# Four reorderings in the attention stages of a one-core gated block: row statistics, bias copies, |w| sums and row normalisation

## The chip, the cores and the metric

The kernel runs on one core of a Trainium2 chip. The metric is the device time of one execution in microseconds (us), as the median of several runs. Engines are named as in the profile: PE (TensorE matmul), PEld (its weight load), DVE (VectorE), ACT (ScalarE), POOL (GpSimd) and SP (SyncE, which here only issues DMAs).

## The reference, cut to what matters

```python
x = x + tanh(g_xattn[0]) * xattn(layernorm(x), ctx, Wq, bq, Wk, bk)
x = x + tanh(g_ffn[0]) * ffn(layernorm(x), W_up, W_gate, W_down)

def xattn(t, ctx, Wq, bq, Wk, bk):        # t: (4, 512, 512), ctx: (4, 512, 256)
    q = einsum('bnc,dc->bnd', ctx, Wq) + bq
    k = einsum('bnc,dc->bnd', ctx, Wk) + bk
    attention = softmax(einsum('bnd,bmd->bnm', q, k), axis=-1)
    return einsum('bln,bmn->blm', t, attention)

def ffn(x, W_up, W_gate, W_down):         # 512 -> 2048 -> 512
    # ternary(w): scale = mean(|w|) + 1e-8; clip(round(w / scale), -1, 1) * scale
    up, gate = x @ ternary(W_up).T, x @ ternary(W_gate).T
    return (silu(up) * gate) @ ternary(W_down).T
```

## The kernel before, in words

There are four batches of 512 rows by 512 columns. A row tile is 128 rows, so a batch has four (NT = 4). Everything up to about 95 us is attention; from there on PE runs the products of the feed-forward part back to back. All five engines have their instructions written out by hand in program order, and semaphores tie them together. What is reordered is therefore only what one engine does next.

Attention of one batch goes like this. `project(b, m)` (L736, PE) makes queries (m = 0) and keys (m = 1) in PSUM. `bias_qk(b, m)` (L1109, ACT) adds the bias and copies them to SBUF. `energy(b, i)` (L750, PE) is one row tile of energies. `row_max` (L1487, DVE), `exp_row` (L1116, ACT), `row_rsum` (L1491, DVE) and `norm_p` (L1121, ACT; in batch 0 tiles 1 to 3 on DVE, L1573, counted by `s_pn0`) make the softmax. `transpose_p` (L761, PE) turns the probabilities round and `copy_at` (L1125, ACT) copies them to SBUF, counted by `s_at`.

The product of x with the attention is done in two ways.

- Batches 0 and 1: by seven block products instead of eight, `mix_product(b, j)` (L800, PE) in the order j = 1, 2, 6, 5, 7, 3, 4, each of four matmuls (eight records). Three of them take blocks as they are (1, 2, 4 on the left side), the others take sums of blocks. POOL makes these sums: four "x sums" (L574 to L583, counted by `s_ss`) and four "attention sums" `p_sum_1` to `p_sum_4` (L587 to L598, counted by `s_ts`). Product 6 needs an x sum and the second attention sum, product 7 an x sum and the third attention sum. `XA` says which x sum a product takes, and so for which count of `s_ss` it waits. `add_mixed(b, j)` (L1521, DVE) scales a product by the row's 1/sigma and adds it to x. PE's product 6 waits for `add_mixed(b, 1)`.
- Batches 2 and 3: plainly, one row tile after another, `mix(b, i)` (L777, PE, four matmuls, which the trace records as eight) and `make_x1(b, i)` (L1509, DVE).

The row statistics of the first layer norm are `bn_stats` and `bn_aggr` on DVE (L1498, L1504, counted by `s_ln1`) and then on POOL `rstd1_two(b, h)` for two row tiles at once (L559 to L563, five small instructions with a wait after each, counted by `s_r1`) or `rstd1(b, i)` for one (L549 to L552). Those of the second layer norm are `stats2`, `aggregate2` (L1529, L1535) on DVE and `rstd2_two` or `rstd2` on POOL (L568, L569; L603, L604). `norm_x1(b, i)` (L1543, DVE) normalises a row tile for the feed-forward part; it waits for `rstd2` of that tile.

Beside this ACT sums |w| over the weights, `sum_abs(m, c)` (L1102, 2048 columns each), as their DMAs land. DVE also makes the low parts of the feed-forward's input, `low_t` (L1561).

The program order before, around the change:

- POOL, batch 0: x sums 0 and 1; then, after `s_pn0` = 3, the third x sum; `p_sum_1`, `rstd1_two(0, 0)`, `p_sum_2`, `rstd1_two(0, 1)`, `p_sum_3`, the fourth x sum, `p_sum_4`; then the x sums of batch 1.
- ACT, batch 0: `copy_at(0, 3)`, `bias_qk(1, 0)`, `bias_qk(1, 1)`, `sum_abs(0, 0)`, `sum_abs(0, 1)`, the exponentials of batch 1's tiles 0 and 1, their two `norm_p`, `sum_abs(0, 2)`, `copy_at(1, 0)`, `exp_row(1, 2)` and so on.
- PE, batch 0: ..., `transpose_p(0, 3)`, product 1, `energy(1, 0)`, `energy(1, 1)`, product 2, product 6, `transpose_p(1, 0)`, `energy(1, 2)`, products 5 and 7, `transpose_p(1, 1)`, `energy(1, 3)`, product 3, ...
- DVE, batch 0: `add_mixed(0, 1)`, `row_max` and `row_rsum` of batch 1's tiles 0 and 1, `add_mixed(0, 2)`, ...
- DVE, batches 2 and 3, for each tile i: `make_x1(b, i)`, `stats2`, `row_max` of the next batch, `aggregate2`, `stats1` of a later tile, `row_rsum`, `aggregate1`, and in batch 2 `norm_x1(2, i)`; then a `low_t` or a subtraction.
- PE, batch 2: `mix(2, 1)`, `transpose_p(3, 0)`, `energy(3, 2)`, `mix(2, 2)`, `transpose_p(3, 1)`, `energy(3, 3)`, `transpose_p(3, 2)`, `mix(2, 3)`, `transpose_p(3, 3)`, then `mix(3, 0)` to `mix(3, 3)`.

`energy(b, 1)` and `transpose_p(0, 3)` use the same PSUM bank.

Of the kernel before, what the change touches and what calls it, by code (L numbers as in the profile page):

```python
# [6 lines left out]
def gated_block_kernel(nc, x, xT, first, ctxT, wqkT, wugT, wdT, x1_dram, out):  # L7
# [19 lines left out]
    NT = ROWS // P  # L27
# [18 lines left out]
    with stack:  # L46
# [207 lines left out]
        XA = {1: (0, 0), 2: (0, 1), 4: (1, 1), 5: 0, 7: 1, 6: 2, 3: 3}  # L254
# [266 lines left out]
        def _(pool):  # L521
# [49 lines left out]
            def x_sums_1(b):  # L571
                for i in range(NT):
                    pool.wait_ge(*xt_in(b, i))
                pool.tensor_tensor(x_sum(b, 0), x_quarter(b, 1, 0), x_quarter(b, 1, 1), ALU.add).then_inc(s_ss, 1)  # L574
                pool.tensor_tensor(x_sum(b, 1), x_quarter(b, 0, 0), x_quarter(b, 1, 0), ALU.subtract).then_inc(s_ss, 1)

            def x_sum_2(b):
                hold(pool, s_ss, 4 * b + 1)
                pool.tensor_tensor(x_sum(b, 2), x_sum(b, 0), x_quarter(b, 0, 0), ALU.subtract).then_inc(s_ss, 1)

            def x_sum_4(b):
                hold(pool, s_ss, 4 * b + 3)
                pool.tensor_tensor(x_sum(b, 3), x_quarter(b, 0, 1), x_sum(b, 2), ALU.subtract).then_inc(s_ss, 1)  # L583
# [41 lines left out]
            x_sums_1(0)  # L625
            hold(pool, s_pn0, NT - 1)
            x_sum_2(0)
            p_sum_1(0)
            rstd1_two(0, 0)
            p_sum_2(0)  # L630
            rstd1_two(0, 1)
            p_sum_3(0)
            x_sum_4(0)
            p_sum_4(0)
            x_sums_1(1)
            x_sum_2(1)
            x_sum_4(1)
# [93 lines left out]
        def _(pe):  # L731
# [8 lines left out]
            def energy(b, i):  # L740
                if b == 0 and i == 0:
                    pe.wait_ge(s_k0, 2)
                    pe.wait_ge(s_q0, 1)
                elif b == 0 and i == 1:
                    pe.wait_ge(s_qk, 2)
                elif i == 0:
                    pe.wait_ge(s_qk, b * 2 + 2)
                if i >= 2 and b > 0:
                    pe.wait_ge(s_exp, b * NT + i - 1)
# [340 lines left out]
        def _(act):  # L1090
# [86 lines left out]
            for b in range(NB):  # L1177
                first, last = b == 0, b == NB - 1
                copy_at(b, NT - 1)
# [4 lines left out]
                else:  # L1184
                    bias_qk(b + 1, 0)
                    bias_qk(b + 1, 1)
                if first:
                    sum_abs(0, 0)
                    sum_abs(0, 1)
# [6 lines left out]
                for i in range(NT):  # L1196
# [25 lines left out]
                    if first and i in (0, NT - 1):  # L1222
                        sum_abs(0, 2 + (i > 0))
# [260 lines left out]
        def _(dve):  # L1484
# [142 lines left out]
            for b in range(NS, NB):  # L1627
                last = b == NB - 1
                for i in range(NT):
# [21 lines left out]
                    if not last:  # L1651
                        norm_x1(b, i)
# [9 lines left out]
                    if last:  # L1662
                        if i == 0:
                            low_t(0, "T2", xf_half(0, 0))
# [308 lines left out]
```

## Time and profile before

| what | us |
|---|---|
| median of 3 runs | 396.75 (396.34 to 397.29) |
| the profiled execution, its own time | 397.67 |
| its span, first to last instruction | 395.9 |
| PE busy in the span | 390.0 |
| DVE / ACT / POOL busy | 314.5 / 266.7 / 170.4 |

The profiled execution took 0.9 us more than the median, and 1.8 us of its time lie outside the span. Busy time of PE is modelled from the starts of its matmuls, so a group's end reaches into the next one's start; what PE loses is best read as the distance between starts.

### The profile page before, as it was taken

The page shows a single profiled execution, that of the slowest core. Times are in us where ns is not written, and L with a number is a line of the kernel's source. Part 1 is how long each engine was busy: PE and PEld are TensorE (multiplying, and loading weights), DVE is VectorE, ACT ScalarE, POOL GpSimd, SP SyncE. Part 2 cuts the span into 40 slices and gives each one's busy share as a digit, 9 for nine tenths or more (in the row PEclk, how much of TensorE's full clock was granted, in tenths as well). Part 3 has the DMA queues.
Part 4 walks back from the last instruction along what each step waited for, and adds up shares of the span by engine and source line. Part 5 has one row for each costly group of instructions (what it writes and reads, how often), then busy time and mean ns, then how long its engine had stood idle before and what let it go on. Part 6 is the DMA issues. An engine that isn't in the chain of part 4 may idle for free.

```text
span 395.9 us, 6059 instructions
## 1 busy us (share of the span) xinstructions
PE 390.0 (99%) x1944; PEld 214.8 (54%) x1952; DVE 314.5 (79%) x475; ACT 266.7 (67%) x360; POOL 170.4 (43%) x187
## 2 busy tenths in 40 slices
PE   8999999999999999999999999999999999999997
PEld 6567775454444444444444444444445565656886
DVE  0768898788889985779897875786869989798974
ACT  3796989789778686868887863746377566654400
POOL 0487826658985014222337001535359446271000
PEclk9999999999999999999999999999999999999999
DMA  7999967599600030030009643041500000000014
GB/s 278 410 412 415 392 208 161 150 270 224 157 9 0 1 108 0 0 108 0 2 0 219 117 81 65 1 160 74 170 23 1 2 2 2 0 2 0 2 54 160
DMA packets 43183, 43.91 MB, mean 111 GB/s; under 512 B 30992, under 2 KB 33168, under 8 KB 41104
## 3 DMA queue, kind: packets, MB, share of 16 engines
q1 hardware_dynamic: 43152, 43.53, 35.6%
q8 instruction: 16, 0.26, 0.3%
q14 instruction: 15, 0.12, 0.1%
HBM read 29.89 MB, written 6.29 MB: 91 GB/s over the span
## 4 chain that ended last, share of the span: by engine, by line
PE 82%; ACT 6%; DVE 4%; issue 4%; POOL 3%; DMA 1%; DVEq 0%; POOLq 0%; ACTq 0%
PE pair L886 23%; PE pair L888 22%; PE pair L960 14%; PE pair L1004 11%; PE pair L777 4%; PE pair L800 2%; PE pair L750 2%; PE pair L736 2%; ACT sh L1116 1%; PE pair L761 1%; PE pair L815 1%; DMA xf<-in_first 1%; DVE x_sb L1521 1%; ACT sh L1121 1%; DVE small L1487 1%
## 5 line engine op out<-in xcount | busy, mean ns | idle before, releaser
L886 PE MATMUL pair<-xb_hi,w_sb 128*128 128x512 f16 x448 | 169.8, 379 | 0.2 <-DVE xf L1683 0.2
L888 PE MATMUL pair<-xb_lo,w_sb 128*128 128x512 f16 x448 | 169.8, 379 | 0.0
L886 PEld LDWEIGHTS pair<-xb_hi,w_sb 128*128 128x128 bf16 x448 | 43.8, 98 | 52.4 <-ACT xf L1313 0.7
L888 PEld LDWEIGHTS pair<-xb_lo,w_sb 128*128 128x128 bf16 x448 | 43.9, 98 | 51.2 <-issue 0.3
L1264 ACT ACTIVATE xf<-xf,small 128x512 f32<-128x512 f32 x48 | 34.5, 720 | 52.4 <-DVE xf L1683 31.6
L960 PE MATMUL pair<-x_sb,sh 128*128 128x512 bf16 x248 | 55.0, 379 | 0.4
L1688 DVE SCALAR_TENSOR_TENSOR xf<-xf,small 128x512 f32<-128x512 f32 x48 | 40.1, 837 | 8.4 <-ACT xf L1264 8.3
L960 PEld LDWEIGHTS pair<-x_sb,sh 128*128 128x128 f16 x256 | 24.9, 98 | 30.6 <-DVE x_sb L1725 0.8
L610 POOL TENSOR_TENSOR w_sb<-w_sb 128x512 bf16<-128x512 bf16 x8 | 9.6, 1196 | 63.1 <-ACT w_sb L1138 63.1
L1693 DVE TENSOR_TENSOR sh<-xf,sh 128x512 f16<-128x512 f32 x36 | 32.1, 900 | 0.7 <-ACT sh L1275 0.7
L1739 DVE SCALAR_TENSOR_TENSOR x_sb<-pair,small,x_sb 128x256 f32<-128x256 f32 (+1 forms) x57 | 25.6, 475 | 5.9 <-PE pair L1004 5.4
L1725 DVE SCALAR_TENSOR_TENSOR x_sb<-pair,small,x_sb 128x512 f32<-128x512 f32 x32 | 23.9, 748 | 7.8 <-PE pair L960 7.7
L1275 ACT ACTIVATE sh<-xf 128x512 f16<-128x512 f32 x36 | 22.1, 623 | 10.4 <-DVE xf L1688 9.2
L709 POOL TENSOR_TENSOR xf<-xf 128x512 f32<-128x512 f32 x7 | 9.8, 1406 | 44.2 <-DMA xb_lo<-xf 28.1
L777 PE MATMUL pair<-sh,xt_sb 128*128 128x512 f32 (+2 forms) x80 | 28.6, 509 | 0.0
L1678 DVE TENSOR_TENSOR xf<-pair,xf 128x1024 f32<-128x1024 f32 x16 | 19.5, 1221 | 8.8 <-PE pair L888 8.6
L1683 DVE TENSOR_TENSOR xf<-pair,xf 128x1024 f32<-128x1024 f32 x16 | 19.5, 1221 | 4.1 <-PE pair L888 3.9
L1673 DVE TENSOR_TENSOR xf<-pair,xf 128x1024 f32<-128x1024 f32 x16 | 19.5, 1221 | 4.1 <-issue 1.6
L1301 ACT ACTIVATE xf<-pair 128x1024 f32<-128x1024 f32 x16 | 16.4, 1022 | 8.1 <-PE pair L888 7.7
L777 PEld LDWEIGHTS pair<-sh,xt_sb 128*128 128x128 f32 x80 | 13.9, 190 | 12.6 <-issue 10.5
L1688 DVE SCALAR_TENSOR_TENSOR c<-c,small,pair 128x512 f32<-128x512 f32 x16 | 11.9, 742 | 10.1 <-ACT c L1264 10.1
L1132 ACT ACTIVATE w_sb<-w_sb,small 128x1024 f32<-128x1024 f32 x16 | 18.9, 1227 | 0.0
(198 smaller groups left out, 717.3 us busy)
## 6 DMA issues: line engine op xcount, KB each, us to landing
w_sb<-in_wugT SPq DMA_DIRECT2D x8, 1024.0 KB, 15.4
x_sb<-in_x SPq DMA_DIRECT2D x4, 1024.0 KB, 11.6
xf<-in_wdT SPq DMA_DIRECT2D x4, 1024.0 KB, 6.6
xt_sb<-in_wdT SPq DMA_DIRECT2D x4, 1024.0 KB, 5.2
xt_sb<-in_xT SPq DMA_DIRECT2D x12, 256.0 KB, 6.3
x_dram<-x_sb SPq DMA_DIRECT2D x8, 256.0 KB, 3.4
out<-x_sb SPq DMA_DIRECT2D x8, 256.0 KB, 2.0
x_sb<-x_dram SPq DMA_DIRECT2D x2, 1024.0 KB, 5.5
```

Source lines behind the costliest of these rows:

```text
L777: last = pe.matmul(ps_x[i % 2][:, lo:hi], xt_tile(b, i)[:, k, :], at[:, k, lo:hi], start=(k == 0), stop=(k == KD - 1))
L886: pe.matmul(dst[:, m * 512:(m + 1) * 512], w[:, o:o + P], hi[:, k], start=start and k == 0, stop=False, skip_group_check=not start)
L888: last = pe.matmul(dst[:, m * 512:(m + 1) * 512], w[:, o:o + P], lo[:, k], start=False, stop=k == 1, skip_group_check=not start)
L960: ins = pe.matmul(dst, h_part(n, c, lo)[:, i * P:(i + 1) * P], t_d[:, e * DM + lo_col:e * DM + hi_col], start=first and n == units[0] and ...
L1004: ins = pe.matmul(fin_bank(g, j, t), hidden(u, c, lo, min(t, NT - 1)), cols, start=first and u == units[0] and lo == 0 and not (side and t ...
L1264: act.activation(cb(n, c)[:, 0:512], src, ACT.Silu, scale=su[:, :]).then_inc(s_silu[c], 1)
L1275: act.activation(part(n, c, 0), shaped(n, c, cb(n, c)[:, 0:512]), ACT.Copy).then_inc(s_hi[c], 1)
L1673: dve.tensor_tensor(cb(n, "11"), ps_y[:, :], cb(n, "11"), ALU.add).then_inc(s_c["11"], 1)
L1688: dve.scalar_tensor_tensor(cb(n, c)[:, 0:512], cb(n, c)[:, 0:512], kap[:, :], gate, ALU.mult, ALU.mult).then_inc(s_mul[c], 1)
L1693: dve.tensor_tensor(part(n, c, 1), shaped(n, c, cb(n, c)[:, 0:512]), part(n, c, 0), ALU.subtract)\
L1725: dve.scalar_tensor_tensor(y_tile(b, i), at, c_out[:, :], y_tile(b, i), ALU.mult, ALU.add)\
L1739: dve.scalar_tensor_tensor(fin_rows(g, j, t), fin_bank(g, j, t), c_out[:, :], fin_rows(g, j, t), ALU.mult, ALU.add).then_inc(s_ef, 1)
```

## The change

Four things are moved. Nothing is computed that was not computed before.

1. POOL, batch 0: `rstd1_two(0, 0)` stands ahead of `p_sum_1(0)` instead of behind it. The four x sums are split into four functions: the difference of the two plain blocks, which was second, is now third, and in batch 0 it is done behind `rstd1_two(0, 1)` instead of at the very beginning. `XA` and the semaphore counts follow the new order. In batch 1 the same four sums stand in the new order.
2. ACT, batch 0: both `bias_qk(1, m)` stand ahead of `copy_at(0, 3)`. Because of the shared PSUM bank PE waits at `energy(1, 1)` for `s_at` = 4.
3. ACT, batch 0: `sum_abs(0, 1)` moves from ahead of the exponentials of batch 1's tiles 0 and 1 to behind their `norm_p`, where it stands ahead of `sum_abs(0, 2)`.
4. DVE, batch 2: `norm_x1(2, i)` is done one tile later, at the place of tile i + 1; the last one in batch 3 at tile 0.

```diff
--- before.py
+++ after.py
@@ -251,7 +251,7 @@
         MIX = (1, 2, 6, 5, 7, 3, 4)
         MIX_TO = {1: (0, 0), 5: (1, 1), 6: (0, 1), 3: (0, 1), 7: (1, 1), 2: (0, 0), 4: (1, 0)}
         MIX_BEFORE = {2: 1, 3: 6, 7: 5}
-        XA = {1: (0, 0), 2: (0, 1), 4: (1, 1), 5: 0, 7: 1, 6: 2, 3: 3}
+        XA = {1: (0, 0), 2: (0, 1), 4: (1, 1), 5: 0, 6: 1, 7: 2, 3: 3}
         PB = {1: (0, 0), 2: (1, 0), 3: (1, 1), 5: 0, 6: 1, 7: 2, 4: 3}
 
         def x_quarter(b, lh, nh):
@@ -568,19 +568,21 @@
                 step(pool.tensor_scalar(ve2[:, two], mv2[:, own, 1], LN_EPS, 1.0 / XS ** 2, ALU.add, ALU.mult))
                 pool.tensor_tensor(r2[:, own], ve2[:, two], mhalf, ALU.pow).then_inc(s_r2, 2)
 
-            def x_sums_1(b):
+            def x_sum_1(b):
                 for i in range(NT):
                     pool.wait_ge(*xt_in(b, i))
                 pool.tensor_tensor(x_sum(b, 0), x_quarter(b, 1, 0), x_quarter(b, 1, 1), ALU.add).then_inc(s_ss, 1)
-                pool.tensor_tensor(x_sum(b, 1), x_quarter(b, 0, 0), x_quarter(b, 1, 0), ALU.subtract).then_inc(s_ss, 1)
 
             def x_sum_2(b):
                 hold(pool, s_ss, 4 * b + 1)
-                pool.tensor_tensor(x_sum(b, 2), x_sum(b, 0), x_quarter(b, 0, 0), ALU.subtract).then_inc(s_ss, 1)
+                pool.tensor_tensor(x_sum(b, 1), x_sum(b, 0), x_quarter(b, 0, 0), ALU.subtract).then_inc(s_ss, 1)
+
+            def x_sum_3(b):
+                pool.tensor_tensor(x_sum(b, 2), x_quarter(b, 0, 0), x_quarter(b, 1, 0), ALU.subtract).then_inc(s_ss, 1)
 
             def x_sum_4(b):
-                hold(pool, s_ss, 4 * b + 3)
-                pool.tensor_tensor(x_sum(b, 3), x_quarter(b, 0, 1), x_sum(b, 2), ALU.subtract).then_inc(s_ss, 1)
+                hold(pool, s_ss, 4 * b + 2)
+                pool.tensor_tensor(x_sum(b, 3), x_quarter(b, 0, 1), x_sum(b, 1), ALU.subtract).then_inc(s_ss, 1)
 
             def p_sum_1(b):
                 hold(pool, s_at, b * NT + NT)
@@ -622,18 +624,20 @@
 
             pool.wait_ge(s_tanh, 1)
             pool.wait_ge(s_const, 4)
-            x_sums_1(0)
+            x_sum_1(0)
             hold(pool, s_pn0, NT - 1)
             x_sum_2(0)
+            rstd1_two(0, 0)
             p_sum_1(0)
-            rstd1_two(0, 0)
             p_sum_2(0)
             rstd1_two(0, 1)
+            x_sum_3(0)
             p_sum_3(0)
             x_sum_4(0)
             p_sum_4(0)
-            x_sums_1(1)
+            x_sum_1(1)
             x_sum_2(1)
+            x_sum_3(1)
             x_sum_4(1)
             rstd1_two(1, 0)
             rstd2_two(0, 0)
@@ -745,6 +749,8 @@
                     pe.wait_ge(s_qk, 2)
                 elif i == 0:
                     pe.wait_ge(s_qk, b * 2 + 2)
+                if b == 1 and i == 1:
+                    pe.wait_ge(s_at, NT)
                 if i >= 2 and b > 0:
                     pe.wait_ge(s_exp, b * NT + i - 1)
                 pe.matmul(e_bank(b, i), q_sb[:, i * P:(i + 1) * P], k_sb, start=True, stop=True).then_inc(s_e, 1)
@@ -1176,17 +1182,19 @@
 
             for b in range(NB):
                 first, last = b == 0, b == NB - 1
+                if first:
+                    bias_qk(1, 0)
+                    bias_qk(1, 1)
                 copy_at(b, NT - 1)
                 if last:
                     act.activation(warm[:, :], tanh_sb[:, :], ACT.Silu)
                     sign_unit(0)
                     sum_abs(2, 3)
-                else:
+                elif not first:
                     bias_qk(b + 1, 0)
                     bias_qk(b + 1, 1)
                 if first:
                     sum_abs(0, 0)
-                    sum_abs(0, 1)
                 elif not last:
                     if b == 1:
                         sum_abs(1, 0)
@@ -1219,8 +1227,11 @@
                             act.wait_ge(s_t1, 1)
                             high_t(0, "T1", xf_half(1, 0))
 
-                    if first and i in (0, NT - 1):
-                        sum_abs(0, 2 + (i > 0))
+                    if first and i == 0:
+                        sum_abs(0, 1)
+                        sum_abs(0, 2)
+                    if first and i == NT - 1:
+                        sum_abs(0, 3)
                     if b == 1:
                         if i == 0:
                             sum_abs(1, 2)
@@ -1648,8 +1659,8 @@
                         row_rsum(b + 1, i + 1)
                     if more:
                         aggregate1(nb, ni, mark1)
-                    if not last:
-                        norm_x1(b, i)
+                    if not last and i > 0:
+                        norm_x1(b, i - 1)
                     if b == 2:
                         if i == 1:
                             low_t(0, "T3", t3_sb)
@@ -1661,6 +1672,7 @@
                             dve.tensor_tensor(xf_half(0, 0), t3_sb, xf_half(0, 0), ALU.add).then_inc(s_t2, 1)
                     if last:
                         if i == 0:
+                            norm_x1(b - 1, NT - 1)
                             low_t(0, "T2", xf_half(0, 0))
                         if i == 1:
                             low_t(0, "B22", xf_half(1, 1))
```

## Rows read from the trace of the kernel before

**Rows 1.** The page of the profile, busy time of each engine.

```profile
PE 390.0 (99%) x1944; PEld 214.8 (54%) x1952; DVE 314.5 (79%) x475; ACT 266.7 (67%) x360; POOL 170.4 (43%) x187
```

**Rows 2.** Timeline of PE, attention of batches 0 and 1: start, length, what, idle.

```profile
17.79 1.89 PE L800 MATMUL pair<-sh,xt_sb 128*128 128x256 f32 x8
19.79 1.98 PE L750 MATMUL pair<-sh 128*128 128x512 f32 x4
...
23.66 1.97 PE L800 MATMUL pair<-xf 128*128 128x256 f32 x8 [0.16 <-POOL xf L591]
26.07 0.66 PE L761 MATMUL pair<-early,sh 128*128 128x128 f32 x4 [0.44 <-ACT sh L1121]
26.56 1.02 PE L750 MATMUL pair<-sh 128*128 128x512 f32 x2
...
39.94 1.89 PE L800 MATMUL pair<-sh,xb_lo 128*128 128x256 f32 x8
...
47.27 1.02 PE L750 MATMUL pair<-sh 128*128 128x512 f32 x2
```

**Rows 3.** Timeline of PE, attention of batches 2 and 3.

```profile
66.01 3.60 PE L777 MATMUL pair<-sh,xt_sb 128*128 128x512 f32 x8
...
70.74 3.60 PE L777 MATMUL pair<-sh,xt_sb 128*128 128x512 f32 x8
...
74.61 1.02 PE L750 MATMUL pair<-sh 128*128 128x512 f32 x2
...
75.91 3.60 PE L777 MATMUL pair<-sh,xt_sb 128*128 128x512 f32 x8
80.25 0.66 PE L761 MATMUL pair<-early,sh 128*128 128x128 f32 x4 [0.74 <-ACT sh L1121]
80.75 10.51 PE L777 MATMUL pair<-sh,xt_sb 128*128 128x384 f32 x32
```

**Rows 4.** Timeline of POOL, first batch.

```profile
16.06 1.27 POOL L579 TENSOR_TENSOR xf<-xf,xt_sb 128x512 f32<-128x512 f32 x1 [2.76 <-DVE sh L1573]
18.73 1.27 POOL L587 TENSOR_TENSOR xf<-sh 128x512 f32<-128x512 f32 x1 [1.40 <-ACT sh L1125]
20.08 0.19 POOL L559 TENSOR_SCALAR small<-small 128x2 f32<-128x2 f32 x1
...
22.24 1.28 POOL L591 TENSOR_TENSOR xf<-sh,xf 128x512 f32<-128x512 f32 x1
```

**Rows 5.** Timeline of ACT, first batch.

```profile
17.98 0.60 ACT L1125 ACTIVATE sh<-pair 128x512 f32<-128x512 f32 x1 [1.45 <-PE pair L761]
...
19.62 1.92 ACT L1102 ACTIVATE xb_hi<-w_sb 128x2048 f16<-128x2048 f32 x1
...
23.96 0.69 ACT L1116 ACTIVATE sh<-pair,small 128x512 f32<-128x512 f32 x1 [0.44 <-DVE small L1487]
```

**Rows 6.** Timeline of DVE, first batch.

```profile
17.43 0.18 DVE L1504 BATCH_NORM_AGGREGATE small<-small 128x2 f32<-128x6 f32 x1
...
22.39 0.88 DVE L1521 SCALAR_TENSOR_TENSOR x_sb<-pair,small,x_sb 128x256 f32<-128x256 f32 x2 [3.05 <-POOL small L563]
```

**Rows 7.** Timeline of POOL beside the third batch.

```profile
70.96 0.63 POOL L550 TENSOR_TENSOR small<-small 128x1 f32<-128x1 f32 x1
...
75.23 1.34 POOL L550 TENSOR_TENSOR small<-small 128x1 f32<-128x1 f32 x1
```

**Rows 8.** Timeline of DVE, third and fourth batch.

```profile
70.63 0.55 DVE L1543 TENSOR_SCALAR xf<-x_sb,small 128x512 f32<-128x512 f32 x1 [2.07 <-POOL small L604]
71.09 0.74 DVE L1509 SCALAR_TENSOR_TENSOR x_sb<-pair,small,x_sb 128x512 f32<-128x512 f32 x1
...
74.95 1.22 DVE L1561 TENSOR_TENSOR xb_lo<-t_sb,xb_hi 128x1024 f16<-128x1024 f32 x1
...
95.33 0.75 DVE L1509 SCALAR_TENSOR_TENSOR x_sb<-pair,small,x_sb 128x512 f32<-128x512 f32 x1
```

**Rows 9.** Timeline of ACT, end of the third batch.

```profile
79.48 0.72 ACT L1121 ACTIVATE sh<-sh,small 128x512 f32<-128x512 f32 x1
```

## Prediction

> **What bounds the kernel now.** I read the page first. PE is busy for 99% of the span [rows 1], so only what lets PE lose less can help, and the question is where PE loses anything. The list of PE's waits names few; all but the one at the start lie between 23 and 81 us, where this change is made. Because the ends of matmuls are modelled, I then read the loss from distances between starts in PE's timeline.
>
> Batches 0 and 1 run the same sequence: product 1, two energies, product 2, product 6, a transpose, the next energy. In batch 1 it takes 47.27 - 39.94 = 7.33 us without a wait, in batch 0 it takes 26.56 - 17.79 = 8.77 us [rows 2]. So batch 0 loses 1.44 us. Its parts: a product or an energy pair takes (7.33 - 0.44) / 4 = 1.72 us (0.44 for a transpose is my estimate, the 0.49 from 26.07 to 26.56 less a little for its start after a wait), so the energies at 19.79 come 0.28 late; the transpose and what is marked at it and at product 6 make the rest.
>
> In batch 2 a mix, a transpose and the start of the next energy take 74.61 - 70.74 = 3.87 us; the same from 75.91 (mix, transpose, start of the next mix) takes 80.75 - 75.91 = 4.84 us [rows 3]. That is 0.97 us lost, waiting for `norm_p(3, 3)` [rows 9]. Together 2.41 us can come back.
>
> **The bias copies.** The energies at 19.79 wait for both `bias_qk(1, m)`, which stand behind `copy_at(0, 3)`; ACT had idled 1.45 us before that copy [rows 5]. Moved ahead, the first copy of the biases fits into that idle time, the second must wait for its projection, which ends at about 17.5, just before product 1's first matmul [rows 2]; both are done by 18.2, `copy_at(0, 3)` by 18.8 instead of 18.6. PE wants the energies at 17.79 + 1.72 = 19.51. The new wait for `s_at` = 4 at `energy(1, 1)` is met at 18.8, so it costs nothing; all of PE stands behind it, and it would cost only if the copy came after 20.4. Gain: the 0.28 us.
>
> **The statistics ahead of the sums.** POOL idled 1.40 us before `p_sum_1`, from 17.33 on [rows 4]. `rstd1_two(0, 0)` needs only the second tile's aggregate, ready at 17.43 + 0.18 = 17.61 [rows 6]; with 0.16 us of hand-over (my estimate, the size of the waits tagged in rows 2) it starts at 17.77 instead of 20.08. From its first instruction to the next function is 22.24 - 20.08 = 2.16 us, to DVE's `add_mixed(0, 1)` 22.39 - 20.08 = 2.31 us [rows 4, 6]. So:
>
> - `add_mixed(0, 1)` starts at 20.08 (product 1 ended by then). The exponential follows 23.96 - 22.39 = 1.57 us later [rows 5, 6], at 21.65, and PE's transpose 26.07 - 23.96 = 2.11 us after that, ready at 23.76.
> - `p_sum_1` starts at 17.77 + 2.16 = 19.93, a good us after `copy_at(0, 3)` has let it, and takes 1.27; with 0.14 for the wait on itself `p_sum_2` starts at 21.34, ends at 22.62 and reaches PE 0.14 later (22.24 + 1.28 against 23.66), at 22.76.
> - PE wants product 6 at 17.79 + 3 x 1.72 = 22.95 and the transpose at 24.67. Both are met, with 0.2 and 0.9 us in hand.
>
> So the whole 1.44 us comes back. What is late next is product 7. PE wants it at 24.67 + 0.44 + 0.86 + 1.72 = 27.69 (half a pair for one energy). POOL: `p_sum_2` ends at 22.62, the second `rstd1_two` takes 2.16 and about 0.1 of start, then the moved x sum and `p_sum_3` at 1.24 to 1.27 each: done at 27.4, at PE by 27.5. It also holds, by 0.2 us. Before, this x sum had been done in POOL's first idle time, so it now costs POOL 1.25 us that the 1.1 us saved in front pay for; batch 1's sums are needed only after 40 us and hide that.
>
> If a small POOL instruction stretches, both margins go. The nearest rows are the same one-column power at 0.63 and at 1.34 us [rows 7], 0.71 more. One such stretch ahead of product 6 costs 0.71 - 0.2 = 0.5 us; two ahead of product 7 cost 1.42 - 0.2 = 1.2 us, which is the bound above. Below, nothing: POOL cannot give PE more than PE can take. I take no stretch, since the row of 1.34 ran beside DVE's `low_t` [rows 7, 8], and in 17.8 to 27.5 DVE runs `bn_stats`, `row_max` and `add_mixed`, no such subtraction.
>
> The Trainium skill (SBUF — State Buffer, section "SBUF: two separate sides") says that DVE and GpSimd share a port pair that one of them holds for a whole instruction, DVE only in its two-port modes or with two SBUF inputs; by that rule the two stretches would be 0 and the sum as I have it. The pair of rows at 75 us agrees (1.34 us beside a subtraction of two SBUF operands).
>
> **The |w| sum behind the exponentials.** It runs 1.92 us plus 0.2 for its read-out [rows 5]. Before, two such sums stood ahead of the exponentials. With the exponential wanted at 21.65 the second, started at 20.6, would have held ACT until 22.7; moved, it isn't in the way. It and `sum_abs(0, 2)` then fill ACT from 24.3 to 28.2; behind them are queued `copy_at(1, 0)`, the third exponential and its `norm_p`, done by 31. PE wants them at the third transpose, 27.69 + 1.72 + 0.44 + 0.86 + 1.72 = 32.4. Cost nothing, with 1.4 us of cover.
>
> **The later normalisation.** DVE idled 2.07 us ahead of `norm_x1(2, 0)`, waiting for POOL's `rstd2`; `make_x1(2, 1)` stood behind it at 71.09 [rows 8]. Without it, it can start when `mix(2, 1)` ends, 66.01 + 3.60 = 69.61 [rows 3]: 1.44 us earlier (69.65). The chain behind it on DVE and ACT (statistics, `row_max`, exponential, `low_t`) is as long as before, one norm standing in each round as it did, so `norm_p(3, 3)` starts at 79.48 - 1.44 = 78.04 and ends at 78.76. PE wants its transpose 3.43 us after 75.91, at 79.34. Gain 0.97 us, with 0.5 in hand. (Times of this paragraph are on the old axis; all of it lies 1.44 earlier by then.) The fourth batch has one norm more, 71.09 - 70.63 = 0.46 us; DVE brings 1.44 with it, so `make_x1(3, 3)`, now at 95.33, still follows PE's last mix, which comes 0.97 earlier. If DVE gained only 0.5 net, product 3 of the first feed-forward unit, which hangs on it by two ACT copies and shows no slack that I can measure from a wait, would take back up to 0.5 us.
>
> **The sum.** 1.44 + 0.97 = 2.41 us. Against the profiled execution's 397.67 us that is 395.3 (span 393.5); the median is 0.92 us below it: 396.75 - 2.41 = 394.34. I say 394.4.
>
> **Rivals.**
>
> - *POOL late:* a stretched power costs 0.5 to 1.2 us at products 6 or 7. For it: margins of only 0.2 us, and a row of 1.34. Against it: no `low_t` on DVE there. Time 394.9 to 395.6.
> - *The stall at the third batch stays*, or moves to `make_x1(3, 3)`: DVE is then bound by something else than the norm. For it: DVE was 79% busy. Against it: 2.07 us of idle time are marked. Only 1.44 come: 395.3.
> - *No change:* both gains are met by waits next in line, or the shift is taken up by the |w| and x loads, which come at fixed times of the DMA queues. Against it: batch 1 ran its sequence without loss, and ACT and DVE found those loads landed. 396.75, within 0.8.
> - *Slower, one mechanism:* POOL's sums of 512 columns themselves stretch now that they meet DVE at other moments. If the four from `p_sum_1`'s start to product 7 took 1.27 + 0.71 us, product 7 would come 4 x 0.71 - 0.2 = 2.6 us late, and products 3 and 4 behind two more sums another 1.4 us: 396.75 - 2.41 + 4.0 = 398.3. It decides from 0.6 us of stretch per sum on. Against it: all sums in rows 4 take 1.27 or 1.28.
>
> **How the numbers follow.** The measurement tells 0.2% (0.8 us) from no change. Chances: full gain 0.58, POOL late 0.15, third-batch stall stays 0.11, no change 0.10, slower 0.06. The first three hold 0.84; they reach from 394.34 less half the runs' spread (0.45) to 395.6. Range 393.9 to 395.7. Faster by over 0.2% (under 395.96): 0.84; within: 0.10; slower: 0.06.
>
> **What would show it.** In PE's timeline of the changed kernel the batch-0 sequence should take 7.3 to 7.4 us, and the mix before `transpose_p(3, 3)` to the next mix 3.9. POOL's L559 should start near 17.8, DVE's first L1521 near 20.1, ACT's first exponential of batch 1 near 21.7, L1509 of tile (2, 1) right after the mix. The prediction is wrong if PE shows a wait for POOL's L591 or L594, if L1138 to L1313 on ACT or L1509 on DVE hold up PE near 100 us, or if PE's first feed-forward product does not start 2.4 us earlier than now.

## The result and the profile after

The changed kernel takes 394.2 us (393.69 to 394.87) against 396.75 us (396.34 to 397.29), each the median of 5 runs: ratio 0.9935, 95% interval 0.9917 to 0.9953, so 2.55 us less, with 2.41 worked out and 394.4 predicted. Its profiled execution took 393.74 us, with a span of 391.9. Line numbers from L574 on differ by a few from before's (L604 is L606, L736 is L740, L750 is L756, L761 is L767, L777 is L783, L800 is L806, L1102 is L1108, L1109 is L1115, L1116 is L1122, L1121 is L1127, L1125 is L1131, L1313 is L1324, L1487 is L1498, L1504 is L1515, L1509 is L1520, L1521 is L1532, L1543 is L1554, L1561 is L1572; for POOL, L579 is L578, L587 is L589, L591 is L593, L594 is L596).

The page's busy times, the row that answers to [rows 1]:

```profile
PE 388.1 (99%) x1952; PEld 214.4 (55%) x1952; DVE 315.7 (81%) x475; ACT 266.5 (68%) x360; POOL 168.6 (43%) x187
```

PE's timeline in the changed kernel, batches 0 and 1, then the third batch:

```profile
16.44 1.89 PE L806 MATMUL pair<-sh,xt_sb 128*128 128x256 f32 x8
18.17 1.88 PE L756 MATMUL pair<-sh 128*128 128x512 f32 x4
...
21.61 1.89 PE L806 MATMUL pair<-xf 128*128 128x256 f32 x8
23.34 0.60 PE L767 MATMUL pair<-early,sh 128*128 128x128 f32 x4
23.77 1.02 PE L756 MATMUL pair<-sh 128*128 128x512 f32 x2
...
73.12 3.60 PE L783 MATMUL pair<-sh,xt_sb 128*128 128x512 f32 x8
76.56 0.60 PE L767 MATMUL pair<-early,sh 128*128 128x128 f32 x4
76.99 1.46 PE L783 MATMUL pair<-sh,xt_sb 128*128 128x384 f32 x4
```

Against [rows 2]: product 1 to the next energy takes 23.77 - 16.44 = 7.33 us, where it took 8.77. No row of the sequence carries a wait any more. Against [rows 3]: the mix at 73.12, a transpose and the start of the next mix take 76.99 - 73.12 = 3.87 us, where they took 4.84. Both stretches are now as long as their undisturbed twins. That is 1.44 + 0.97 = 2.41 us. PE's first feed-forward product starts 90.99 - 16.44 = 74.55 us behind product 1, where it started 94.75 - 17.79 = 76.96 us behind it: again 2.41 us, so no part of the gain is lost on the way there, and no PE row of the sequence or of the third batch names POOL.

The profiled spans differ by 4.0 us, so 1.6 are not the change's. 1.35 of them are the start: product 1 begins at 16.44 instead of 17.79. In the fourteen executions profiled here it began anywhere from 16.44 to 17.80. The two profiles of the unchanged kernel before have 17.79 and 17.75, but variants of it, with the same PE program, also began at 16.78 to 17.00, and variants of the changed kernel at up to 17.80. PE's timeline shows where the 1.35 come from, first in the changed kernel, then in the kernel before:

```profile
3.85 2.21 PE L821 MATMUL pair<-xf 128*128 128x256 f32 x8
```

```profile
3.98 3.42 PE L815 MATMUL pair<-xf 128*128 128x256 f32 x8
```

It is the same work, the first half of the first projections, and PE has been busy since 0.97 us. Before, its weight loads took 335 ns each (median), in the changed kernel 192. PE runs the beginning at half its later pace, with starts of 256-column records 0.43 us apart instead of 0.22, and over the profiles this ends anywhere from 4 to 7 us. The profile lists the granted clock as 1.00 there all the same, so it doesn't name the cause. The first energies start at 9.10 before and 7.75 here, and that is the 1.35.

Distances from product 1's start can be compared, absolute times can't. The last 0.2 lie in the feed-forward part, and I come back to them.

POOL, first batch, against [rows 4]:

```profile
16.30 0.20 POOL L559 TENSOR_SCALAR small<-small 128x2 f32<-128x2 f32 x1 [0.45 <-DVE small L1515]
...
18.47 1.27 POOL L589 TENSOR_TENSOR xf<-sh 128x512 f32<-128x512 f32 x1
19.89 1.27 POOL L593 TENSOR_TENSOR xf<-sh,xf 128x512 f32<-128x512 f32 x1
...
24.64 1.28 POOL L596 TENSOR_TENSOR xf<-sh 128x512 f32<-128x512 f32 x1
```

ACT, first batch and end of the third, against [rows 5] and [rows 9]:

```profile
16.20 0.69 ACT L1115 ACTIVATE sh<-pair,small 128x512 f32<-128x512 f32 x1 [0.44 <-PE pair L740]
16.79 0.59 ACT L1131 ACTIVATE sh<-pair 128x512 f32<-128x512 f32 x1
...
20.19 0.69 ACT L1122 ACTIVATE sh<-pair,small 128x512 f32<-128x512 f32 x1 [0.93 <-DVE small L1498]
...
22.77 1.90 ACT L1108 ACTIVATE xb_lo<-w_sb 128x2048 f16<-128x2048 f32 x1
...
75.25 0.72 ACT L1127 ACTIVATE sh<-sh,small 128x512 f32<-128x512 f32 x1
```

DVE, first and third batch, against [rows 6] and [rows 8]:

```profile
18.62 0.88 DVE L1532 SCALAR_TENSOR_TENSOR x_sb<-pair,small,x_sb 128x256 f32<-128x256 f32 x2 [0.77 <-POOL small L563]
...
66.86 0.75 DVE L1520 SCALAR_TENSOR_TENSOR x_sb<-pair,small,x_sb 128x512 f32<-128x512 f32 x1 [1.09 <-PE pair L783]
```

Measured from product 1's start, the prediction and the rows compare so:

| step | predicted | measured |
|---|---|---|
| `rstd1_two(0, 0)`, first instruction | -0.02 | 16.30 - 16.44 = -0.14 |
| `add_mixed(0, 1)` | 2.29 | 18.62 - 16.44 = 2.18 |
| first exponential of batch 1 | 3.86 | 20.19 - 16.44 = 3.75 |
| second attention sum done, with hand-over | 4.97 | 19.89 + 1.27 + 0.14 - 16.44 = 4.86 |
| product 6 | 5.16 | 21.61 - 16.44 = 5.17 |
| third attention sum's margin at product 7 | 0.2 | 21.61 + 1.73 + 0.43 + 0.86 + 1.73 - (24.64 + 1.28 + 0.14) = 0.3 |
| last `norm_p` of the third batch to PE's transpose | 0.5 (its times give 79.34 - 78.76 = 0.58) | 76.56 - (75.25 + 0.72) = 0.6 |

The second projection's bias copy starts at 16.20, 0.24 ahead of product 1, and `copy_at(0, 3)` follows at 16.79; the energies at 18.17 come 1.73 behind product 1, with nothing lost. `make_x1(2, 1)` (66.86) now waits for PE's mix, and for nothing of POOL's.

### The profile page after: what moved, and what is told of

It reads as the page before. It is cut to its first block, busy times and chain, and to the rows that moved or that the text cites. A ratio compares the mean times of both kernels' runs of the same rounds, so it can differ in the third digit from the quotient of the medians.

```text
span 391.9 us, 6067 instructions
## 1 busy us (share of the span) xinstructions
PE 388.1 (99%) x1952; PEld 214.4 (55%) x1952; DVE 315.7 (81%) x475; ACT 266.5 (68%) x360; POOL 168.6 (43%) x187
## 4 chain that ended last, share of the span: by engine, by line
PE 94%; DVE 2%; issue 2%; ACT 1%; POOL 0%; DVEq 0%; POOLq 0%; ACTq 0%
PE pair L892 23%; PE pair L894 23%; PE pair L966 14%; PE pair L1010 11%; PE pair L783 7%; PE pair L806 6%; PE pair L756 4%; PE pair L740 3%; PE pair L767 2%; PE pair L817 1%; DVE xf L1700 1%; PE pair L821 1%; DVE x_sb L1751 0%; PE pair L825 0%; POOL xf L717 0%
## 5 line engine op out<-in xcount | busy, mean ns | idle before, releaser
L966 PE MATMUL pair<-x_sb,sh 128*128 128x512 bf16 x256 | 56.6, 379 | 0.0
L783 PE MATMUL pair<-sh,xt_sb 128*128 128x512 f32 (+2 forms) x80 | 28.6, 509 | 0.0
L783 PEld LDWEIGHTS pair<-sh,xt_sb 128*128 128x128 f32 x80 | 13.9, 190 | 12.6 <-issue 10.5
```

Source lines behind the costliest of these rows:

```text
L783: last = pe.matmul(ps_x[i % 2][:, lo:hi], xt_tile(b, i)[:, k, :], at[:, k, lo:hi], start=(k == 0), stop=(k == KD - 1))
L966: ins = pe.matmul(dst, h_part(n, c, lo)[:, i * P:(i + 1) * P], t_d[:, e * DM + lo_col:e * DM + hi_col], start=first and n == units[0] and ...
```

## The experiments

What follows are runs of variants. The first four ran on one chip, where the kernel before took 396.75 us (29 runs); the next four on another (397.63, 9 runs); the last four on a third (396.52, 29 runs). Each was timed in five rounds beside the kernel before. "Sequence" is from product 1's start to `energy(1, 2)` (8.77 before, 7.33 after), "third batch" from the mix ahead of `transpose_p(3, 3)` to the next mix (4.84 and 3.87).

### One edit alone, or all but one

**Only the later normalisation**, on the kernel before:

```diff
-                    if not last:
-                        norm_x1(b, i)
+                    if not last and i > 0:
+                        norm_x1(b, i - 1)
...
+                            norm_x1(b - 1, NT - 1)
                             low_t(0, "T2", xf_half(0, 0))
```

> The kernel before with edit 4 alone (the third batch's rows normalised a tile later). Theory (the two stalls are separate and each edit removes its own): PE from the mix before transpose_p(3, 3) to the next mix takes 3.87 us instead of 4.84, the batch-0 sequence stays at 8.77, the time falls by 0.97 us. Rival (the gain of the third batch hangs on the earlier first batch): the 4.84 stays or only partly goes, the time falls by less than 0.4 us.

Measured: 396.22 us, ratio 0.9986 [0.9978, 0.9995]; third batch 3.87, sequence 9.06. So 0.53 us (0.2 to 0.9) instead of 0.97. The third batch came out as expected, the sequence longer by 0.3.

**All but the later normalisation** (the same lines turned back in the changed kernel).

> The changed kernel with norm_x1 of the third batch back in its old place. Theory: batch-0 sequence 7.33 us, the stall before transpose_p(3, 3) is back (4.84 instead of 3.87), 1.44 us faster than before and 0.97 slower than the changed kernel. Rival (an earlier first batch alone frees POOL enough): the stall at the third batch is below 0.5 us.

Measured: 394.83 us, 0.9958 [0.9941, 0.9974]; sequence 7.34, third batch 78.39 - 74.32 = 4.07. The third batch lost 0.20 us, not 0.97, without the edit that was to cure it: the number that the rival had named. Whether for its reason, the last group of runs tells.

**Only POOL's new order**, with its x sums and `XA`, on the kernel before (the lines of the x sums and of `XA` are left out here):

```diff
...
+            rstd1_two(0, 0)
             p_sum_1(0)
-            rstd1_two(0, 0)
             p_sum_2(0)
             rstd1_two(0, 1)
+            x_sum_3(0)
             p_sum_3(0)
```

> The kernel before with edit 1 alone (POOL's statistics ahead of the sums, x sums reordered). Theory (each of edits 1 to 3 removes one wait of the batch-0 sequence): add_mixed(0, 1) comes 2.3 us earlier, but ACT is held by the second |w| sum until 23.4, so the transpose comes only 0.5 us earlier: sequence 8.2 to 8.3 us, time 0.5 us lower. Rival (the statistics were all of it): sequence 7.6 us (only the 0.28 of the bias copies left), time 1.2 us lower.

Measured: 396.35 us, 0.9985 [0.9976, 0.9994]; sequence 9.20, third batch 4.82. The sequence is neither the 8.2 to 8.3 of the theory nor the 7.6 of the rival, but longer than before.

**All but POOL's new order** (POOL's program and `XA` of before in the changed kernel).

> The changed kernel with POOL's program of before (edits 2, 3 and 4 kept). Theory (POOL's order carries the batch-0 gain): add_mixed(0, 1) waits for POOL as before, the sequence takes 8.8 to 8.95 us (0.17 more than before since copy_at(0, 3) comes later), only the 0.97 of the third batch remains: time 0.8 to 1.0 us below before. Rival (ACT's order carries it): sequence under 8.0 us, time 1.7 us or more below.

Measured: 396.71 us, 0.9998 [0.9988, 1.0007]; sequence 8.92, third batch 3.87. Its PE timeline:

```profile
23.60 1.97 PE L802 MATMUL pair<-xf 128*128 128x256 f32 x8 [0.68 <-POOL xf L591]
26.01 0.66 PE L763 MATMUL pair<-early,sh 128*128 128x128 f32 x4 [0.44 <-ACT sh L1123]
```

With the statistics back behind the first sum, product 6 waits for POOL again and the transpose for ACT, though bias copies and |w| sum stand in their new places. The sequence is as expected. The profile also shows most of the expected gain: from product 1's start to the start of PE's last matmul it takes 374.00 us, against 375.01 and 374.74 in the two profiles of the kernel before. The median of its 11 runs does not: it is 0.04 us below before's where 0.8 to 1.0 were expected, and no profile says why.

The edits don't add up. Alone, normalisation and POOL order bring 0.53 and 0.40 us by the medians (0.56 and 0.60 by the ratios), both with a sequence *longer* than before's 8.77. ACT's timelines say what ended it. Only the normalisation, then only POOL's order (whose L1106 is before's L1102, L765 is L761, L804 is L800, L754 is L750):

```profile
21.57 1.91 ACT L1102 ACTIVATE xb_lo<-w_sb 128x2048 f16<-128x2048 f32 x1 [0.73 <-DMA w_sb<-in_wugT]
```

```profile
21.70 1.91 ACT L1106 ACTIVATE xb_lo<-w_sb 128x2048 f16<-128x2048 f32 x1 [0.87 <-DMA w_sb<-in_wugT]
```

And PE in the same two:

```profile
17.00 1.89 PE L800 MATMUL pair<-sh,xt_sb 128*128 128x256 f32 x8
...
26.06 1.02 PE L750 MATMUL pair<-sh 128*128 128x512 f32 x2
```

```profile
16.99 1.89 PE L804 MATMUL pair<-sh,xt_sb 128*128 128x256 f32 x8
...
25.70 0.66 PE L765 MATMUL pair<-early,sh 128*128 128x128 f32 x4 [1.27 <-ACT sh L1125]
26.19 1.02 PE L754 MATMUL pair<-sh 128*128 128x512 f32 x2
```

In both, ACT stood still ahead of the second |w| sum, not for an engine but for the DMA of its block of weights, and the exponentials were queued behind that sum. In the profile of the kernel before, product 1 began 0.8 us later, and the block had landed by the time ACT came to it. The next group tests this.

### One part of the first batch turned back

**The second |w| sum ahead of the exponentials again**, all else as changed:

```diff
                 if first:
                     sum_abs(0, 0)
+                    sum_abs(0, 1)
...
                     if first and i == 0:
-                        sum_abs(0, 1)
                         sum_abs(0, 2)
```

> The changed kernel with sum_abs(0, 1) back ahead of the exponentials of batch 1. The prediction's working: ACT is held 1.05 us longer than the exponential wants, the transpose comes 0.14 us late, sequence 7.5 us. Theory from the changed kernel's trace: the transpose has 1.1 us in hand and the sum takes 0.9 of it, so sequence 7.33 us and the same time as the changed kernel, 2.4 us faster than before. Rival (the |w| sum is what held the exponential): sequence 8 us or more.

Measured: 396.1 us, 0.9964 [0.9951, 0.9976]; sequence 26.24 - 17.05 = 9.19, third batch 3.87. ACT and PE:

```profile
21.74 1.91 ACT L1108 ACTIVATE xb_lo<-w_sb 128x2048 f16<-128x2048 f32 x1 [1.85 <-DMA w_sb<-in_wugT]
```

```profile
17.05 1.89 PE L806 MATMUL pair<-sh,xt_sb 128*128 128x256 f32 x8
...
25.75 0.66 PE L767 MATMUL pair<-early,sh 128*128 128x128 f32 x4 [1.56 <-ACT sh L1127]
26.24 1.02 PE L756 MATMUL pair<-sh 128*128 128x512 f32 x2
```

1.86 us of sequence are lost, where the prediction's working gave 0.14 and the theory of this run nothing. It is the rival, 8 us or more, and more than everything that the change gains in this batch. ACT waited 1.85 us for the landing, and the transpose 1.56 us for ACT. By time it costs less: 0.6 to 1.2 us, from 0.9964 here against 0.9948 and 0.9935 for the changed kernel on other chips. A profile is one execution, and how much the landing costs depends on how early product 1 starts.

**The bias copies behind `copy_at(0, 3)` again:**

```diff
-                if first:
-                    bias_qk(1, 0)
-                    bias_qk(1, 1)
                 copy_at(b, NT - 1)
+                if first:
+                    bias_qk(1, 0)
+                    bias_qk(1, 1)
```

> The changed kernel with both bias_qk(1, m) back behind copy_at(0, 3). Theory: the energies behind product 1 come 0.28 us late and nothing else moves: batch-0 sequence 7.6 us, 2.1 us faster than before. Rival (the slack of POOL absorbs nothing, but PE's wait is hidden because product 6 waits anyway): sequence 7.33 us.

Measured: 394.99 us, 0.9940 [0.9927, 0.9952]; third batch 3.88. PE:

```profile
17.80 1.89 PE L806 MATMUL pair<-sh,xt_sb 128*128 128x256 f32 x8
19.80 1.98 PE L756 MATMUL pair<-sh 128*128 128x512 f32 x4
21.62 1.89 PE L806 MATMUL pair<-sh,xt_sb 128*128 128x256 f32 x8
...
25.51 1.02 PE L756 MATMUL pair<-sh 128*128 128x512 f32 x2
```

The energies start 2.00 us behind product 1 instead of 1.73, and nothing makes it good later: sequence 7.71, 0.38 us more. 0.27 of it are the late start. The other 0.11 arise right behind it: the pair of energies, started after a wait, takes 21.62 - 19.80 = 1.82 us to the next product instead of 1.71 (19.88 - 18.17 in the changed kernel). In time the loss does not show: 0.9940 lies between the two ratios of the changed kernel, 0.9935 and 0.9948.

**The x difference in POOL's first idle time again**, and only `rstd1_two(0, 0)` moved ahead of `p_sum_1`. The x sums and `XA` are those of the kernel before in both batches; edits 2, 3 and 4 stay. POOL's program against the kernel before:

```diff
             x_sum_2(0)
+            rstd1_two(0, 0)
             p_sum_1(0)
-            rstd1_two(0, 0)
             p_sum_2(0)
             rstd1_two(0, 1)
```

> The changed kernel with the difference of two plain x blocks back in POOL's first idle time (and the x sums in their old order in both batches), the statistics still ahead of the attention sums. Theory: the sums for product 7 are ready 1.2 us earlier, which nobody waits for: sequence 7.33 us, time as the changed kernel, 2.4 us faster than before. Rival (product 7 has no slack): PE gains up to 0.2 us more there.

Measured: 394.11 us, 0.9917 [0.9903, 0.9930]; sequence 7.33, as in the changed kernel. So in the changed kernel POOL's margin at product 7 was enough.

**The moved x sum (1.24 us) between the statistics and `p_sum_1`:**

```diff
             rstd1_two(0, 0)
+            x_sum_3(0)
             p_sum_1(0)
             p_sum_2(0)
             rstd1_two(0, 1)
-            x_sum_3(0)
             p_sum_3(0)
```

> The changed kernel with one x sum (1.24 us of POOL) put between the statistics and p_sum_1, to use up POOL's slack at product 6. Theory (POOL's margin there is 0.3 us by the changed kernel's trace): PE waits 0.9 us at product 6, sequence 8.25 us, 1.5 us faster than before. Rival (POOL is not near the path): sequence 7.33 us.

Measured: 395.16 us, 0.9945 [0.9932, 0.9959]. PE:

```profile
16.59 1.89 PE L806 MATMUL pair<-sh,xt_sb 128*128 128x256 f32 x8
...
22.90 1.97 PE L806 MATMUL pair<-xf 128*128 128x256 f32 x8 [0.98 <-DVE x_sb L1532]
...
25.14 1.02 PE L756 MATMUL pair<-sh 128*128 128x512 f32 x2
```

Product 6 starts 22.90 - 16.59 = 6.31 us behind product 1 instead of 5.17, so it is 1.14 late (the mark says 0.98, because it counts from a modelled end). POOL was 1.24 us later for the x sum, and 0.23 more because its statistics began 0.09 behind product 1 in this execution and not 0.14 ahead of it; less the margin of 0.3 of the table above, that is 1.17. The mark names DVE's `add_mixed`, which had been done by 19.87; what came late was POOL's `p_sum_2`, from 21.49 for 1.27 us, and 0.14 of hand-over: 22.90. The sequence takes 25.14 - 16.59 = 8.55 us, 0.3 more than expected.

### Both kernels again, and the power on POOL

`all_but_norm` raised a question: why did the third batch lose 0.20 us instead of 0.97? The chain back from its `norm_x1(2, 0)` leads over POOL's `rstd2(2, 0)`, which stands behind two subtractions (L651, L653), to a two-column power on POOL, L569. The kernel before, POOL and DVE:

```profile
61.47 1.95 POOL L569 TENSOR_TENSOR small<-small 128x2 f32<-128x2 f32 x1
```

```profile
61.65 1.22 DVE L1561 TENSOR_TENSOR xb_lo<-xf,xb_hi 128x1024 f16<-128x1024 f32 x1
```

All but the normalisation, POOL and DVE:

```profile
59.89 0.81 POOL L569 TENSOR_TENSOR small<-small 128x2 f32<-128x2 f32 x1
```

```profile
60.06 1.22 DVE L1572 TENSOR_TENSOR xb_lo<-xf,xb_hi 128x1024 f16<-128x1024 f32 x1
...
68.27 0.55 DVE L1554 TENSOR_SCALAR xf<-x_sb,small 128x512 f32<-128x512 f32 x1 [1.30 <-POOL small L606]
```

The same power took 1.95 us in one and 0.81 in the other, beside the same `low_t` on DVE, which by the records starts 0.18 or 0.17 us after it. DVE then idles 1.30 us ahead of `norm_x1(2, 0)` instead of the 2.07 of [rows 8], and PE loses 0.20 instead of 0.97. Three of the remaining four runs ask whether that is the edit's doing; the last returns to the |w| sum.

**The kernel before and the changed kernel, each unchanged.**

> The kernel before, unchanged, for a second look. Theory (two things vary from execution to execution: the start of product 1, and whether POOL's power at L569 takes 0.8 or 1.95 us beside DVE's low_t): ratio 1.000, the transpose behind product 6 at 25.5 or later however early product 1 starts, since the second |w| block lands at 21.5 to 21.7, and PE from the mix to the next mix 4.84 us if the power took 1.95, about 4.1 if 0.8. Rival (the losses are fixed): batch-0 sequence 8.77 and 4.84 again.

> The changed kernel, unchanged, for its ratio on the same chip as the others of this call. Theory: sequence 7.33 and 3.87 us whatever the start and the power; 2.5 to 3 us faster than before. Rival (the profile of the changed kernel was a lucky one): 1.5 us or less.

Measured: before 396.4 us, 1.0001 [0.9993, 1.0010]; changed 394.42 us, 0.9948 [0.9936, 0.9959], so 2.1 us less. That is less than the 2.5 to 3 us expected and more than the rival's 1.5. Sequences 8.79 and 7.33, third batch 4.07 and 3.87, the power 0.81 us in both:

```profile
61.45 0.81 POOL L569 TENSOR_TENSOR small<-small 128x2 f32<-128x2 f32 x1
```

So the kernel before itself has either power, and a third batch that loses 0.97 or 0.20 us. Product 1 began as late here (17.75) as in its first profile, so an earlier first batch was not what shortened the stall in `all_but_norm`.

This profile shows a second reason for a late product 1, and here POOL's order has a hand in it. POOL and DVE:

```profile
12.23 1.27 POOL L575 TENSOR_TENSOR xf<-xt_sb 128x512 f32<-128x512 f32 x1
```

```profile
12.35 1.43 DVE L1573 TENSOR_SCALAR sh<-sh,small 128x512 f32<-128x512 f32 x1
```

DVE's `norm_p` of batch 0 takes 0.49 us when no sum of POOL's runs beside it. Here it ends 0.28 us behind POOL's x difference, the sum that the change moves away from there. PE's transpose is marked as waiting 0.35 us for it, and product 1 comes 17.75 - 8.48 = 9.27 us behind the first energies instead of 8.69 (17.79 - 9.10). In `only_norm` it is 9.32, in the seven profiles with that sum moved never more than 8.99 (`only_pool`, beside the first x sum). So the change may gain some tenths of a microsecond ahead of product 1 too, in some executions, which neither the prediction nor the distances of this document count; no run isolates it.

With the later normalisation the third batch takes 3.87 whatever the power does: it was 1.94 or 1.95 in four of the eight profiles with that edit.

But the kernel before with the short power does not keep all of its 0.77 us. PE in that run, and in the one without the later normalisation:

```profile
100.64 0.38 PE L888 MATMUL pair<-xb_lo,w_sb 128*128 128x512 f16 x1
101.24 0.39 PE L886 MATMUL pair<-xb_hi,w_sb 128*128 128x512 f16 x1 [0.22 <-ACT xf L1313]
```

```profile
99.08 0.38 PE L894 MATMUL pair<-xb_lo,w_sb 128*128 128x512 f16 x1
99.66 0.39 PE L892 MATMUL pair<-xb_hi,w_sb 128*128 128x512 f16 x1 [0.20 <-ACT xf L1324]
```

In both PE waits at product 3 of the first feed-forward unit for an ACT copy. The two starts are 0.60 and 0.58 us apart, where such starts are 0.22 apart without a wait, so the wait costs 0.38 and 0.36 us: half of the 0.77. From the first feed-forward product to PE's last matmul it takes 298.54 and 298.50 us, against 298.05 in the first profile of before and 297.87 in the changed kernel. More than the wait itself can't be read from these totals, because they vary by as much for the changed kernel alone: in its second profile the feed-forward part took 298.37 us. 0.3 us of that lie at product 3 of the second unit, where PE's weight load shows this:

```profile
110.93 0.10 PEld L892 LDWEIGHTS pair<-xb_hi,w_sb 128*128 128x128 bf16 x1 [0.63 <-ACT xf L1324]
```

**The `low_t` moved behind two normalisations**, on the kernel before, to take it away from the power:

```diff
                     norm_x1(1, 1)
-                    low_t(0, "B21", xf_half(0, 1))
                     norm_x1(1, 2)
                     norm_x1(1, 3)
+                    low_t(0, "B21", xf_half(0, 1))
```

> The kernel before with one swap on DVE, low_t(0, B21) behind norm_x1(1, 2) and norm_x1(1, 3), so that no subtraction of two SBUF operands runs beside the power at L569. Theory (the power is blocked by that subtraction, and its 1.1 us pass to rstd2(2, 0) and to the third batch): L569 takes 0.7 to 0.8, DVE idles 1.3 us or less ahead of norm_x1(2, 0), the stall before transpose_p(3, 3) is 0.2 us or less, time 0.3 to 0.8 us below before. Rival (the two lengths of the power have another cause): L569 at 1.95 here too, stall 0.97.

Measured: 397.32 us, 1.0018 [1.0009, 1.0027]; third batch 4.52. POOL and DVE:

```profile
60.62 0.81 POOL L569 TENSOR_TENSOR small<-small 128x2 f32<-128x2 f32 x1
62.68 3.22 POOL L651 TENSOR_TENSOR t_sb<-xf 128x1024 f32<-128x1024 f32 x1 [1.25 <-DVE xf L1543]
```

```profile
62.46 1.22 DVE L1561 TENSOR_TENSOR xb_lo<-xf,xb_hi 128x1024 f16<-128x1024 f32 x1
...
69.47 0.55 DVE L1543 TENSOR_SCALAR xf<-x_sb,small 128x512 f32<-128x512 f32 x1 [1.77 <-POOL small L604]
```

The power is short, as expected, but the subtraction now beside `low_t` takes 3.22 us where its sister behind it (same size) took 2.36. The third batch loses 0.65 us, not 0.2 or less. A stretch went with `low_t` to a place no better, which ties the stretches to this DVE instruction. The short power proves little by itself, since the kernel before has it too in some executions. It does show that 0.81 us is what this power takes without `low_t` beside it, so in the executions with 0.81 `low_t` cost it nothing. The median is 0.8 us above before's, where 0.3 to 0.8 below were expected; the profile does not explain that.

**Only the |w| sum moved**, on the kernel before.

```diff
                 if first:
                     sum_abs(0, 0)
-                    sum_abs(0, 1)
...
-                    if first and i in (0, NT - 1):
-                        sum_abs(0, 2 + (i > 0))
+                    if first and i == 0:
+                        sum_abs(0, 1)
+                        sum_abs(0, 2)
+                    if first and i == NT - 1:
+                        sum_abs(0, 3)
```

> The kernel before with edit 3 alone (the second |w| sum behind the exponentials). Theory (in the kernel before the exponential waits for the later of two: DVE's add_mixed, 4.6 us behind product 1, and the landing of the second |w| block at a fixed time): the landing no longer matters, so the batch-0 sequence takes 8.77 us for an early start too, and the time falls by 0 to 0.6 us. Rival (the sum is hidden in the kernel before): no change at all, the transpose comes at 25.5 us or later as in only_norm.

Measured: 396.47 us, 0.9999 [0.9987, 1.0010]. Its profile is of a late start (product 1 at 17.79), in which the landing doesn't matter: sequence 8.77, as before. No gain alone, in a range of 0.5 us either way; the expected shortening in an early execution was not profiled.

## Why the prediction held, point by point

- **The distance method and the sum** (1.44 + 0.97 = 2.41): shown for the profiled executions. The rows give 7.33 and 3.87 us; the two timings give 2.55 and 2.1. That one profile's sum fits the medians so well is in part luck, because both terms change from execution to execution. With an early start and the short power the rows give 9.06 - 7.33 = 1.73 us for the first batch (`only_norm`), 0.20 for the third and 0.4 at product 3, together 2.3 (my estimate; no single execution shows all three). One term grows as the other shrinks.
- **The bias copies** (0.28): shown in the rows, by their removal 0.38; in time no difference shows. The term was mis-sized by 0.10: I had counted the late start of the energies alone, and the pair that starts after the wait also runs 0.11 longer, in the kernel before too (21.61 - 19.79 = 1.82).
- **The statistics ahead of the sums:** shown. Without this, 8.92. Every time in the table is within 0.12 us of its forecast. The margins were 0.3 where I had 0.2, and 1.24 us more of POOL's work ahead of product 6 cost the rest at once (`xsum_between`). No power stretched in the first batch (0.71 or 0.72 us for two columns in all rows read), so the rival of a late POOL fell.
- **The |w| sum behind the exponentials:** the direction right, the term mis-sized and its reason wrong. I had taken the second sum to start when ACT was free, at 20.6, and put 0.14 us on it. In four profiles it began when its block landed, at 21.21, 21.57, 21.70 and 21.74, and the next energy came 4.50, 4.49, 4.49 and 4.50 us later (25.71, 26.06, 26.19, 26.24). Such a constant distance over four kernels says that this landing alone set the energy. In an early execution it costs 1.86 us. So the first batch of the kernel before ended at the later of two times: 8.77 us after product 1 by way of POOL's statistics, or 4.5 us after the landing. In my profile, with product 1 at 17.79, the first one bound, and the second lay hidden at least 0.5 us below it (ACT took the block at 21.51, without a wait, and 21.51 + 4.50 = 26.01 against 26.56). Moving only one of the two leaves the other: hence nothing by time for the |w| sum alone, 0.4 for POOL's order alone, and 1.44 in the rows for both with the bias copies. It also means that the program of before gives away part of an early start (17.00 instead of 17.79, 0.79 us earlier, became 26.06 instead of 26.56, 0.50 earlier) and the changed one keeps it.
- **The later normalisation** (0.97): the third batch is at 3.87 in every kernel with it, and `make_x1(2, 1)` waits for PE alone. The 0.97 was one outcome of two: the stall is 0.97 with the power at 1.95 us and 0.20 with 0.81, and in the second case half of the difference is lost again at product 3. I had read it from one profile as if it were fixed. The term measured by time is 0.53 us (0.2 to 0.9) alone and some 0.4 to 0.9 in the whole (0.9958 against 0.9935 and 0.9948, which their intervals don't separate).
- **The warning about product 3** named the right place: PE does wait there in the first unit, but in the kernel before, or without the edit. With it, none of eight profiles shows a wait in the first unit, and one shows it in the second (0.3 us); what held that copy was not followed.
- **Open:** why the kernel with POOL's old order showed no gain by time, with 0.97 us less in the third batch; why `low_behind` is slower by median; what decides between the two lengths of the power; how often each comes in the timed runs, of which one per variant was profiled; what makes the rest of the 0.5 us by which the feed-forward part varies between executions of the changed kernel; and whether the x difference in its old place is better (394.11 us, but not run beside the changed kernel).

## What to carry to other kernels

When PE is at 99%, compare the distances between starts with an undisturbed repeat of the same sequence, and take from that what a reordering can give at most. Then look at what stands second behind each stall: an instruction that waits for a DMA, placed ahead of one on the path, can be the bound in other executions than the one profiled, so ask at what time its data lands and what happens if the kernel gets there 1 us earlier. And don't price the parts of a reordering one by one where two of them lie on the same wait.

## What was not expected of the hardware

POOL's power over two columns took 0.71 or 0.72 us in the first batch, and at L569 either 0.81 or 1.94 to 1.95 us beside a DVE subtraction of 1.22 us that by the records started 0.17 to 0.18 us behind it; the same kernel showed both (1.95 and 0.81 in the two profiles of before). With the subtraction moved away it took 0.81 too. A POOL subtraction of 1024 columns took 3.22 instead of 2.36 us beside the same instruction: 0.86 more, and the power 1.14 more, both less than the 1.22. The Trainium skill (SBUF — State Buffer, section "SBUF: two separate sides") says that one of the two engines holds their shared port pair for a whole instruction, and DVE only in two-port modes or with two SBUF inputs, as here; the sizes of both stretches agree with that. The same section gives the pair to whichever starts first, and by the recorded starts that was POOL for the power, which was held up all the same; the 1024-column subtraction started 0.22 us behind DVE's, as the rule wants. Why the power comes out at either length at the same recorded distance, no run here explains.

It goes the other way too. DVE's `norm_p` of 512 columns (L1573) takes 0.48 to 0.50 us alone. In ten of the fourteen profiles one of them took 0.59 to 1.43 us beside a POOL sum of 512 columns, and always ended 0.27 to 0.30 us behind the end of that sum.

PE's first eight matmul records took 2.00 to 3.55 us, at half pace for a time that differs from one execution to the next, with the granted clock listed as 1.00 throughout. Product 1 started at 16.44 to 17.80, a difference about as large as all runs of one kernel spread (396.13 to 397.70 for the kernel before on one chip).
